# One of the eight low-part subtractions of the first feed-forward stage is computed on VectorE instead of GpSimd

## The reference

```python
x = x + 0.5 * ffn(layernorm(x))
x = x + attn(layernorm(x))        # a state-space scan over time
x = x + 0.5 * ffn(layernorm(x))

# ffn, D_MODEL 512, D_EXPERT 2048, the weights rounded to -1, 0, 1 times a scale
up, gate = x @ wu.T, x @ wg.T
hidden = silu(up) * gate
out = hidden @ wd.T

# attn, E 1024 channels, N 16 states for each
h = h * exp(delta[:, :, None] * A) + (delta * x)[:, :, None] * B[:, None, :]   # for each token
y = einsum('ben,bn->be', h, C)
```

## Time and profile before

| | |
|---|---|
| median of three runs | 2855.8 us |
| profiled execution, span | 2855.8 us, 2854.0 us |
| TensorE busy | 2624.6 us, 92% |
| VectorE busy | 2505.5 us, 88% |
| GpSimd busy | 2431.0 us, 85% |
| ScalarE busy | 1882.4 us, 66% |
| low parts on GpSimd (L903) | 256 instructions, mean 1228 ns |

### The profile page before, as it was taken

How to read it: one execution, slowest core, us unless ns; L and a number is a source line. 1 busy time by engine, 2 the same in 40 slices (tenths; PEclk the granted TensorE clock), 3 DMA queues, 4 the chain that set the end, 5 groups by cost and what they waited for, 6 DMA issues and landing times.

```text
span 2854.0 us, 52248 instructions
## 1 busy us (share of the span) xinstructions
PE 2624.6 (92%) x17415; PEld 2028.3 (71%) x17415; DVE 2505.5 (88%) x3273; ACT 1882.4 (66%) x4368; POOL 2431.0 (85%) x2192
## 2 busy tenths in 40 slices
PE   5766899999999999999999999999999999998868
PEld 4555677776877777786777778687777768776635
DVE  6468899999999999999999999999999999998872
ACT  7275767766676767667676676767677676767531
POOL 1168899999899999999999999999999998999881
PEclk9888899999999999999999999999999999999988
DMA  7012223222222322322222222222232222222230
GB/s 269 30 51 63 62 58 77 58 61 73 61 72 63 77 55 61 78 62 72 64 71 56 68 70 60 73 59 75 58 77 58 61 73 60 71 65 75 49 74 8
DMA packets 95315, 194.45 MB, mean 68 GB/s; under 512 B 12684, under 2 KB 32712, under 8 KB 94536
## 3 DMA queue, kind: packets, MB, share of 16 engines
q0 software_dynamic: 20736, 75.51, 13.7%
q1 hardware_dynamic: 74312, 115.60, 12.6%
HBM read 106.66 MB, written 8.91 MB: 40 GB/s over the span
## 4 chain that ended last, share of the span: by engine, by line
PE 38%; POOL 21%; DVE 20%; issue 11%; ACT 3%; DMA 1%; POOLq 0%; DVEq 0%; ACTq 0%
PE ps L1686 12%; POOL h L802 12%; DVE h L1394 9%; PE ps L1697 9%; PE ps L1709 6%; PE ps L1758 5%; PE ps L1643 5%; POOL h L817 4%; DVE xc L1467 3%; DVE y L1423 2%; POOL hl L903 2%; ACT ps L1058 1%; DVE act L1439 1%; DVE act L1431 1%; POOL delta L869 1%
## 5 line engine op out<-in xcount | busy, mean ns | idle before, releaser
L802 POOL TENSOR_TENSOR h<-u,bb 128x1024 f32<-128x1024 f32 x512 | 1260.3, 2461 | 13.0 <-POOL u L912 4.4
L1394 DVE TENSOR_TENSOR_SCAN h<-ps,h 128x512 f32<-128x512 f32 x1024 | 1190.3, 1205 | 47.6 <-POOL h L806 39.6
L1058 ACT ACTIVATE ps<-delta,a_neg 128x255 f32<-128x255 f32 x2048 | 874.6, 469 | 398.5 <-DVE h L1394 395.1
L1686 PE MATMUL ps<-xh,q_up 128*128 128x256 f16 x2048 | 468.1, 275 | 34.3 <-DVE xl L1308 21.7
L1686 PE MATMUL ps<-xh,q_gate 128*128 128x256 f16 x2048 | 464.2, 274 | 21.8 <-DVE xw L1500 15.6
L1423 DVE SCALAR_TENSOR_TENSOR y<-ps,ccur,y 128x512 f32<-128x512 f32 x672 | 467.6, 737 | 6.0 <-PE ps L1643 5.3
L1686 PE MATMUL ps<-xl,q_up 128*128 128x256 f16 x2048 | 468.0, 275 | 0.0
L1686 PE MATMUL ps<-xl,q_gate 128*128 128x256 f16 x2048 | 464.1, 274 | 0.0
L1643 PE MATMUL ps<-ident,h 128*128 128x128 f32 x2944 | 397.2, 278 | 66.2 <-DVE y L1423 62.9
L1643 PEld LDWEIGHTS ps<-ident,h 128*128 128x128 f32 x2944 | 345.7, 143 | 127.0 <-DVE h L1394 53.6
L1697 PE MATMUL ps<-q_down,hh 128*128 128x512 fp8e4 x1024 | 389.7, 381 | 7.4 <-issue 3.9
(11 more groups left out here) (134 smaller groups left out, 3763.9 us busy)
## 6 DMA issues: line engine op xcount, KB each, us to landing
xw<-h POOLq DMA_DIRECT2D x144, 512.0 KB, 4.5
bb<-b_scratch SPq DMA_DIRECT2D x224, 256.0 KB, 3.1
cplane<-c_scratch SPq DMA_DIRECT2D x144, 128.0 KB, 3.0
xs<-in_L_attn_resid_dram SPq DMA_DIRECT2D x17, 512.0 KB, 3.6
out_dram<-xs SPq DMA_DIRECT2D x15, 512.0 KB, 4.2
wraw<-in_L_ffn_W_up_dram SPq DMA_DIRECT2D x4, 1024.0 KB, 9.5
wraw<-in_L_ffn_W_gate_dram SPq DMA_DIRECT2D x4, 1024.0 KB, 12.2
wraw<-in_L_ffn_W_down_dram SPq DMA_DIRECT2D x4, 1024.0 KB, 14.1
```

The lines of the kernel that those rows point to most:

```text
L802: pl.tensor_tensor(h[:, (STEPS * i + s) % RING, :, :], u[:, :, :], bb[:, q % 2, s % PLANES:s % PLANES + 1, :].broadcast_to([P, HE, CH]), A ...
L1058: ins = ac.activation(abar[r][:, e, 1:], delta[:, k, 1:], ACT.Exp, scale=a_neg[:, k, n:n + 1])
L1394: v.tensor_tensor_scan(hr, abar[r].rearrange("p e t -> p (e t)"), hr, 0.0, ALU.mult, ALU.add).then_inc(scanned, 1)
L1686: ins = te.matmul(pp[:, f * CH:(f + 1) * CH], w[:, d, col:col + P], part[:, d, :], start=(d == 0 and part is xh), stop=(d == DB - 1 and pa ...
```

## The change

One number enters the table. Pair 6 of kind 1 is now computed by VectorE in all chunks, 16 instructions in all (one in fill, one in first, 14 in the loop); the other 240 stay on GpSimd.

```diff
-LOW_ON_DVE = {1: [], 2: []}
+LOW_ON_DVE = {1: [6], 2: []}
```

## The result

The changed kernel takes 2888.86 us (2886.77 to 2891.93, 4 runs) against 2854.83 us of the kernel before (4 runs): ratio 1.012, 95% interval 1.0103 to 1.0138, or 34.0 us more. The forecast was 2891, with a range of 2861 to 2899. The profiled execution took 2884.44 us with a span of 2882.6, 28.6 us more than the span before. It was 2.3 us quicker than the quickest of the four timed runs, which themselves lie 5.2 us apart.

A forecast was written before the change was run, and what follows sets the result against it. VectorE's path, barely later than TensorE's at 1409 us, was taken to bound the kernel. 13 passes x 2.75 = 35.8, plus 0.6 for the fifth, less 1.8, gave +34.6, taken as +35: 2891 us, range 2861 to 2899.

The forecast's parts named there:

- The wait for GpSimd's current instruction: Slot 10: VectorE's new two-SBUF-input instruction waits until GpSimd's whole L802 (2.35 us) is done, then runs alone.
- 2.75 us on VectorE: Slot 10: VectorE's next instruction starts at 1356.81 instead of 1354.06, +2.75 us per pass; bounds 0.59 and 2.94.
- What comes back: On the way to 1409 only VectorE's 0.3 us DMA wait into `xw` is given back, six times, 1.8 us.
- The price without a wait: The moved instruction's own time on VectorE's queue when nothing holds it up: 0.59 us a pass.
- rival A: Slot 10: VectorE gets in before L802, costs only its own 0.59 us a pass, 2861 to 2865 us; chance 0.20.
- The exception: In the fifth loop pass VectorE would take hold before GpSimd's L802, costing 0.6 us instead of 2.75.
- The tie at slot 7: L1400 ties VectorE and GpSimd together each pass, so their distance at slot 10 stays the same in nearly all passes.
- GpSimd's relief is worth nothing: Slot 9: the 1.12 us a pass taken from GpSimd counts 0, since its L834 then waits for VectorE's moments.
- The sign: GpSimd not waiting at L834 for the moments would show that its relief counts; a 2 to 3 us wait was expected.
- TensorE 2.1 us late: TensorE's transposes at 1359.78 wait for y of slot 10; with 0.62 us of slack they come 2.1 us late.
- VectorE has no slack: Between slot 7 and 1409 us VectorE has practically no slack; its path is the later, TensorE being 0.39 us early.

The follow-up runs named there:

- without the masks: Changed kernel with VectorE's mask L1400 issued only where a sequence begins, elsewhere just a semaphore count: 2867.20 us, ratio 1.0044 to the kernel before.
- with pair 1: Kernel before, with the low part of pair 1 instead of pair 6 moved to VectorE, two SBUF inputs: 2876.38 us, ratio 1.0077.

## Why the prediction was right, and where it was off

The result lies 2 us below the forecast, and the cause is the one that was priced. That it lies so near is in part luck: with the changed kernel's four runs 5.2 us apart, the 34.0 us stand for anything from 29.4 to 39.4, and the pair of traces, taken term by term, gives 12 x 2.50 + 0.60 + 0.6 = 31.2 us from the loop on, where the sum had 34.6.

- *The wait for GpSimd's current instruction.* Shown from four sides: it goes with one input in PSUM (2859.8), stays without the work (2880.3), goes when GpSimd is later by 0.2 us (2864.5), and comes back at another length at another place (2876.4). What the instruction's own 0.55 us of data cost is the smaller part.
- *2.75 us on VectorE.* Measured 2.74 in pass 7, and 2.69 on average over the twelve passes with a wait from which the 2.50 come, since in passes 5 and 11 L802 was already 0.31 and 0.43 us under way. Of these 2.69 us the pass keeps 2.50. The term had been sized on VectorE's queue alone and taken over to the pass but for some DMA waits.
- *What comes back.* The sum took 1.8 us back for VectorE's waits for the DMA into `xw`. Over the 13 passes these fell from 1.4 to 0.7 us, and all waits of VectorE above 0.15 us together from 125.2 to 124.0. Another 1.2 us are in gaps and lengths too small to be put down to anything. No run took one of them away by itself.
- *The price without a wait.* 0.59 us a pass in rival A; 0.37 with the input in PSUM, with an interval up to 0.61, and 0.60 in pass 8. No miss is shown here.
- *The exception.* One pass did go the other way, but it was pass 8 and not the fifth, and that the count came out is luck. In pass 8 GpSimd was late by a wait of 0.3 us for a DMA. In the fifth pass L802 was 0.31 us ahead of VectorE, more than elsewhere, and not behind it. L802 had been reckoned to start 0.06 us ahead of VectorE in pass 7, and it was 0.08. Which pass turns round can't be read from the trace before.
- *The tie at slot 7.* Right for most passes: without L1400 nine of the 11 concerned turn round, by a shift of 0.13 us.
- *GpSimd's relief is worth nothing.* Right, 2854.87 us. The place was wrong: I had GpSimd wait at L834 for the moments, and had named GpSimd not waiting there as a sign that its relief counts. In pass 7 nearly all of its wait comes earlier: 3.1 us at the low part of pair 7, for ScalarE's `hh`, which is late with the scans. L834 itself then starts 0.08 us behind the end of the moments (1379.56 against 1379.48), where it had been 0.37, and so 2.5 us later than before, reckoned from the scans of slot 10; 2.4 had been forecast. The sign was badly chosen: the late VectorE can hold GpSimd at any point ahead of L834.
- *TensorE 2.1 us late.* Its transposes of slot 11 start 15.13 us later than in the kernel before (1374.91 against 1359.78), and the scans of slot 10 start 13.08 us later (1364.89 against 1351.81): TensorE is 2.05 us late, as forecast. But most of it is the one new wait of 1.6 us at the transposes of slot 10, and not at those of slot 11, where it had been reckoned.
- *VectorE has no slack.* This holds for a delay and not for a gain. I had called VectorE's path the later one, by 0.39 us. By that, a microsecond taken off at slot 26 should have come out, and nothing did. In the passes that were looked at, TensorE, GpSimd and ScalarE reach the same points within some tenths of a microsecond, so here the added wait counted nearly in full and the one removed turned into others.

## What to carry to other kernels

When work goes from GpSimd to VectorE, count the inputs that lie in SBUF. With two of them the instruction here took the rest of the product that GpSimd was in, and then its own time on top. A forecast of this can be read from the trace before: take the start of the instruction that will stand behind it, and look at what GpSimd is doing then. It is a forecast and no more where the two start within 0.1 us of each other, since a shift of that size turns the outcome round. In a kernel whose engines are balanced to some tenths of a microsecond, test a gain by leaving the work out first: it may be worth nothing while the same amount added costs nearly all of itself (2.50 of 2.69 us a pass here).

## What the runs showed of the hardware

The wait goes both ways and is settled by who starts first: VectorE 0.08 us behind L802 waited for 2.27 us, VectorE 0.06 us ahead of it did not wait, and L802 took 0.48 us longer (pass 7 of the changed kernel and of the one with the additional instruction). The closest cases on either side are 0.05 us behind, in pass 6 of the changed kernel, with the full wait, and 0.01 us ahead, in pass 8 of the run with eight elements, with none.

The wait has an exact end. In the changed kernel, in the runs with the additional instruction and without the masks, and with pair 1, each of the 37 subtractions of 512 elements that met a long product of GpSimd's already under way ended 0.55 us after that product did, whether 0.5 or 2.3 us of it were left. With eight elements it was 0.02 to 0.03 us. So VectorE does not work at all in the meantime, and when the product ends it goes ahead of GpSimd's next instruction, which takes longer by as much (the L806 of 0.54 us in pass 7).

So a kernel became 24 us faster through an instruction of 0.2 us that does nothing. Eight elements with two inputs in SBUF took 2.29 us; 512 elements with one of them in PSUM took 0.66.
